# A macaron block of float32 attentions: the order of the steps is written anew, and the exponentials' scales come from registers

## The reference

```python
x = x + 0.5 * ffn_int(norm(x))       # rows quantised to int8, times a 128x128 int8 weight, plus bias
x = x + attn0(norm(x))               # 16 heads of 8, rotary, causal, one W_O of 128x128
x = x + 0.5 * ffn_int(norm(x))
x = x + 0.5 * ffn_gated(norm(x))     # silu(x Wg) * (x Wu), hidden size 384, then Wd
x = x + attn1(norm(x))               # 16 heads of 64, causal, w_o of 1024x128
x = x + 0.5 * ffn_gated(norm(x))
```

## Time and profile before

| | us |
|---|---|
| median of 3 timed runs | 776.01 |
| the three | 773.67, 776.34, 776.01 |
| span of the profiled execution | 771.9 |
| TensorE busy (PE) | 708.9 (92%) |
| VectorE busy (DVE) | 533.9 (69%) |
| ScalarE busy (ACT) | 460.9 (60%) |
| GpSimd busy (POOL) | 488.1 (63%) |

### The profile page before, as it was taken

The page is one execution under the profiler, slowest core; times in us unless marked ns, Lnnn a source line. Parts: engine busy times, 40 slices in busy tenths (PEclk is TensorE's granted clock), DMA queues, the critical chain, the costliest instruction groups (busy, mean ns, idle before and its releaser), DMA issues.

```text
span 771.9 us, 21579 instructions
## 1 busy us (share of the span) xinstructions
PE 708.9 (92%) x9387; PEld 421.0 (55%) x9387; DVE 533.9 (69%) x730; ACT 460.9 (60%) x544; POOL 488.1 (63%) x387
## 2 busy tenths in 40 slices
PE   2768988988888899999999999999999999999997
PEld 1533535445444464666555565655785655666764
DVE  7599889888988786777957556774446465653137
ACT  2424877987787879555565654745525656764502
POOL 6824546206853400689898889969649778889640
PEclk9855999999999999999999999999999999999999
DMA  8000000000000000001011001110101100111000
GB/s 280 2 1 2 4 1 3 3 2 3 3 2 3 1 3 2 2 3 31 3 29 29 30 3 30 31 30 3 29 3 29 31 4 28 29 31 43 27 18 28
DMA packets 13225, 16.20 MB, mean 21 GB/s; under 512 B 3052, under 2 KB 10572, under 8 KB 13132
## 3 DMA queue, kind: packets, MB, share of 16 engines
q1 hardware_dynamic: 12556, 14.50, 6.5%
q10 hardware_dynamic: 576, 0.33, 0.1%
HBM read 13.26 MB, written 1.17 MB: 19 GB/s over the span
## 4 chain that ended last, share of the span: by engine, by line
PE 73%; DVE 11%; ACT 8%; issue 3%; POOL 3%; DMA 1%; SPq 0%; ACTq 0%; DVEq 0%; POOLq 0%
PE ps L1284 21%; PE ps L1233 17%; DVE big L1097 7%; ACT Pr L714 6%; PE ps L1204 6%; PE ps L1263 6%; PE ps L1450 6%; PE ps L1489 3%; PE ps L1457 3%; PE ps L1294 2%; PE ps L1399 2%; PE ps L1274 1%; PE ps L1244 1%; PE ps L1407 1%; PE ps L1254 1%
## 5 line engine op out<-in xcount | busy, mean ns | idle before, releaser
L714 ACT ACTIVATE Pr<-ps,exp_scale 128x1024 f32<-128x1024 f32 (+1 forms) x284 | 277.0, 1032 | 111.2 <-PE ps L1284 54.8
L696 POOL TENSOR_TENSOR V0s<-V0s,Pr 128x1024 f32<-128x1024 f32 x77 | 181.4, 2356 | 94.4 <-PE ps L1233 58.7
L1128 DVE TENSOR_REDUCE mxb<-ps 128x8 f32<-128x1024 f32 (+1 forms) x152 | 173.6, 1163 | 95.3 <-PE ps L1284 75.1
L1097 DVE TENSOR_REDUCE big<-ps 128x8 f32<-128x1024 f32 (+1 forms) x159 | 170.6, 1117 | 18.4 <-PE ps L1263 15.7
L1284 PE MATMUL ps<-big 64*128 64x128 f16 (+2 forms) x2560 | 169.2, 260 | 0.7 <-ACT Pr L714 0.4
L1263 PE MATMUL ps<-big 32*128 32x128 f16 (+2 forms) x1280 | 104.7, 275 | 33.9 <-DVE big L1097 16.5
L1284 PEld LDWEIGHTS ps<-big 64*128 64x128 f16 x2560 | 93.3, 94 | 73.7 <-issue 23.6
L1233 PE MATMUL ps<-Pr,V1s 128*64 128x128 f32 (+2 forms) x960 | 110.5, 371 | 0.0
L1263 PEld LDWEIGHTS ps<-big 32*128 32x128 f16 x1280 | 42.9, 94 | 107.8 <-ACT Pr L714 43.9
L696 POOL TENSOR_TENSOR acts<-acts,Pr 128x1024 f32<-128x1024 f32 x35 | 83.2, 2378 | 18.7 <-PE ps L1233 8.4
L1204 PE MATMUL ps<-Pr,V0s 128*18 128x128 f32 (+2 forms) x1280 | 77.8, 368 | 0.2 <-ACT Pr L721 0.2
(11 more groups left out here) (246 smaller groups left out, 911.7 us busy)
## 6 DMA issues: line engine op xcount, KB each, us to landing
rec_b<-scratch_dram SPq DMA_DIRECT2D x30, 256.0 KB, 3.9
X<-in_x_dram SPq DMA_DIRECT2D x2, 256.0 KB, 3.5
big<-in_pick_rows_dram SPq DMA_DIRECT2D x2, 256.0 KB, 3.0
X<-in_x_dram SPq DMA_DIRECT2D x1, 512.0 KB, 5.3
rec_b<-in_w_q_dram SPq DMA_DIRECT2D x1, 512.0 KB, 5.8
XT<-in_w_k_dram SPq DMA_DIRECT2D x1, 512.0 KB, 6.6
XT<-in_w_v_dram SPq DMA_DIRECT2D x1, 512.0 KB, 7.4
wo_s<-in_w_o_dram SPq DMA_DIRECT2D x1, 512.0 KB, 8.0
```

What stands on the lines that cost most here:

```text
L696: g.tensor_tensor(dst, dst, src, ALU.add).then_inc(summed, 1)
L714: ins = a.activation(dst[:, part], src, func, scale=scale)
L1097: ins = v.tensor_reduce(maxima_of(mall[:, r, 2 * u:2 * u + 2][:, part], i), block_view(src, i), AX.X, ALU.max, negate=True)
L1128: ins = v.tensor_reduce(maxima_of(mxb[:, r][:, part], arg), block_view(src, arg), AX.X, ALU.max, negate=True)
```

## The change

Three edits.

The string `ORDER` is another one. It has the same letters in the same numbers; each stream's own order is what it was. In the string, uninterrupted runs of `W` are 57 instead of 84, the longest has 7 instead of 6.

Three numbers are loaded from SBUF into registers of ScalarE: the scale of the first attention's exponentials when the first `a` is done, that of the second's and the values' factor at the first weight split. The exponentials and the values' copies take their scale from these registers instead of from the 128 partitions.

Before the first weighing of each pair TensorE also waits for ScalarE's copy of that pair's values; in the new order this copy may stand behind the pair's first exponential.

```diff
 ORDER = (
-    "ammmmmmmmammmmmmmmmmamtmmmeeehemmhhememmmwmhewemewemewemhwmemwememehemwthweahemeweehmwegemwemehmwmem"
-    "emwemwemhmewmmhmemmewhmeeemhmwmmhmmtmhhhmememwmeehmegewemmwhmhehwmemheweamewemmtewemewmemwemeemwmeme"
...
-    "TKWWWMEhEEMWWMMQhVWEMMhWWMEEEEEMWWSMEEWWTVKVhWhMWMEMhWMEEMWWMEEEESEMWWWMEMWWWThWEEEEWWWOOSEEEEEOOWWW"
+    "ammmmmmmmammmmmmmmmmmtammheeemehwmemwhememmehewemewmemwmmwehmememehmemwtheahwmeehwemewemegemewmemwe"
+    "memwmehhmewmmhmememmehwememwmhmthmwmhmhhmememwmehewemgeemhmwhemhwmeehwmeamewememtemwemememwmemwemwem"
...
+    "EEEWMMWWMEEEEEMWWWWWWEMhMWWMMKhQVVSTMEEEEEEEEMWWWWMMMWWWEMMWWMEEMhSTEEEEEEWWWWWWWEEEEEESEEWWOOOOWWWW"
     "WWW"
 )
...
+            exp_by = [a.alloc_register(f"exp_by_{k}") for k in range(2)]
+            v_by = a.alloc_register("v_by")
             copy_heads(0)
...
                 if kind == "wsplit":
                     act.wait_ge(scale_ready, 2)
+                    if key == 0:
+                        a.load(exp_by[1], exp_scale[1][0:1, 0:1].bitcast(I32))
+                        a.load(v_by, v_back[0:1, 0:1].bitcast(I32))
...
                     if key == 0:
                         copy_heads(1)
+                        a.load(exp_by[0], exp_scale[0][0:1, 0:1].bitcast(I32))
...
-                    copy_whole(n, group_buf[e_no % GROUP_BUFS], ACT.Exp, exp_scale[0][:, 0:1])
+                    copy_whole(n, group_buf[e_no % GROUP_BUFS], ACT.Exp, exp_by[0])
...
-                    copy_whole(n, in_banks(V1s[:, key % SETS]), ACT.Copy, v_back[:, 0:1])
+                    copy_whole(n, in_banks(V1s[:, key % SETS]), ACT.Copy, v_by)
...
-                    copy_whole(n, dst, ACT.Exp, exp_scale[1][:, 0:1])
+                    copy_whole(n, dst, ACT.Exp, exp_by[1])
...
                 pe.wait_ge(slot_act, read("A", "exp", p, c))
                 if c == 0:
+                    pe.wait_ge(slot_act, read("A", "pv", p, None))
                     pe.wait_ge(acc1_saved if p else acc0_saved, p or G)
```

More of the change, by code:

```diff
@@ L189 @@
 ORDER = (
-    "ammmmmmmmammmmmmmmmmamtmmmeeehemmhhememmmwmhewemewemewemhwmemwememehemwthweahemeweehmwegemwemehmwmem"
-    "emwemwemhmewmmhmemmewhmeeemhmwmmhmmtmhhhmememwmeehmegewemmwhmhehwmemheweamewemmtewemewmemwemeemwmeme"
[L192 to L198, removed]
-    "TKWWWMEhEEMWWMMQhVWEMMhWWMEEEEEMWWSMEEWWTVKVhWhMWMEMhWMEEMWWMEEEESEMWWWMEMWWWThWEEEEWWWOOSEEEEEOOWWW"
+    "ammmmmmmmmammmmmmmmmmmtammheeemehwmemwhememmehewemewmemwmmwehmememehmemwtheahwmeehwemewemegemewmemwe"
+    "memwmehhmewmmhmememmehwememwmhmthmwmhmhhmememwmehewemgeemhmwhemhwmeehwmeamewememtemwemememwmemwemwem"
+    "amewemewemewememewemewemmeewhmmwtmemwhmegememwemegmahhmmwmheheweehmwmemwemhmheewemewemetmehmemwmemwm"
+    "emhahwememhehewemewemewmememwemwemhemheetwemhhhhhwhhhwhhwhemhemgmehemwemheewhemwememememwemwemwemewm"
+    "mhemwmKQQtVVMegeeMweMeweMeweMeweMeweMeweMeweeMgeewTKKQwwMMgEEEMWMMWWMMVhMEEMEEEEMMWWMMKQhTWWWWhMEhSM"
+    "EhEhMWWMhEEMEEMEMWTEMMWWWWMMEWWhMEVhKQWWMEEMhEEMMWWWWTSMhEEEEhMWMMKVQWWMEEEEMWMMMWWWMESTMEMWMEEEMKhQ"
+    "WWMhhhWWEMEEEMTShhhWWWMhEEEEEVhhhWWWMMMhWhWWMEEEMWWMEEMhQKVSTMhhEEEMWWWWWWMEMWMEMWMEEEhWWMMQKWSTEMEE"
+    "EEMWMMQKVWMMMWWWMEEMEEMMWWMMSTWMEEEEEQVKMMWWWWWWMEEMEEMTSMEEMWWMMMWWWWWMEEEMWWMEEEEEEESTVKOOQOOMMMWW"
+    "WWhWWMEEMQKVVMMWWhWMEEMEEEEMSTMEMWWMMMWWWWMEEKhQWWWMEEMEEMhhhhWWWMEETSMEMWhMMMWWWMEEMVhhQVKhhhWWSTME"
+    "EEEWMMWWMEEEEEMWWWWWWEMhMWWMMKhQVVSTMEEEEEEEEMWWWWMMMWWWEMMWWMEEMhSTEEEEEEWWWWWWWEEEEEESEEWWOOOOWWWW"
     "WWW"
```

## The result

The changed kernel takes 770.39 us in the median of eight runs, beside 776.02 for eight runs of the kernel before. One of the eight, of 828.18 us at a mean granted clock of 0.83 instead of 0.96, is left out of the ratio; the other seven lie between 764.92 and 772.6, with a median of 768.7. The ratio is 0.9911, with a 95% interval of [0.9889, 0.9933]: 6.9 us less, where 8.5 were forecast (767.5). The profiled execution has a span of 765.6 us, 6.3 less than before.

What follows compares the result with a forecast made beforehand. TensorE was taken to bound the pair attention, with no engine full in the group attention; -4.7 - 3.2 - 0.3 - 1.0 + 0.2 + 0.5 = -8.5 us from 776.0 gave 767.5 us, range 761.5 to 774.

Steps and rivals of the forecast that it cites:

- Shape changes, pair stage: Pair attention: 49 fewer changes of tile shape on TensorE at 0.096 us each, 4.7 us saved, wholly on the path.
- No new waits: Pair attention: the new order's longer runs of E and M open no waits on TensorE; 0, bound 2 us.
- rival (b): Pair attention: GpSimd's adds become the bound, ScalarE waits at six places, 15 us, giving 782.5 us; chance 0.05.
- Registers: ScalarE's scale from a register saves 94 ns per exponential: 3.2 us in the group attention, hidden in the pair stage.
- The offset of 4.1 us: The profiled span, 771.9 us, lies 4.1 below the timed median of 776.0, which includes what lies around the span.
- Group order: Group attention: 0.3 us from 8 fewer shape changes, 1.0 from fewer bank waits (bounds -3 and +4).
- Tail: Last pair: GpSimd's seven adds, 17.6 us against TensorE's 17.3, end late, so the last sum waits: +0.5 us.
- Loads: Three loads into ScalarE's registers, one early and two at the group attention's first weight split: +0.2 us, from 0 to 3.4.
- (a): Rival: ScalarE's saving buys nothing, by the register form's cost or VectorE's maxima ending last; 771.5 us, chance 0.22.
- (d): Rival: the register form costs 94 ns more per exponential instead of less; 778 us, no change, chance 0.08.
- (e): Rival: the order buys nothing on TensorE, the shape-change surcharge being a wait that only moves; 772.2 us, chance 0.04.
- (c): Rival: the group stage gains 6 us beyond the sum from faster exponentials and the order together; 761.5 us, chance 0.11.

Runs made afterwards that it cites:

- registers only: The kernel before with its old order, plus the three loads and scales from registers; 769.94 us, ratio 0.9924.
- Before, again: The kernel before, unchanged, run once more for a second trace; 775.53 us (one run).
- the swaps: Registers and old order, with W and the M behind it exchanged at 20 pair-stage points, 39 more shape changes; 776.73 us, ratio 1.0003.
- tail mended: Registers, old group order, new pair order, with the last pair's first two weighings moved ahead of its last two score products; 768.18 us, ratio 0.9899.
- three places mended: That mended-tail kernel, plus the ninth pair's sum three steps later and a projection behind two weighings; 769.30 us, ratio 0.9911.
- the order alone: The new order with scales still read from the partitions, against the kernel before; 779.04 us, ratio 1.0037.

## Why the prediction came out right, point by point

The total was forecast well (8.5, measured 6.9), partly because errors of its terms cancelled. Beside the forecast of registers -3.0 and order -5.5 stand, from kernels of one group, registers -6.1 and order -1.0.

- **Shape changes, pair stage: right mechanism, sized too low.** Forecast 49 x 0.096 = 4.7 us; measured 0.12 to 0.14 each, 6.1 to 6.6. The surcharge I read was that between the last matmul of one shape and the first of the next. The weighing behind a change is itself slower: counted over the trace of the pair stage, in weighings of four matmuls of 512 columns, the median from the first to the last is 0.487 us, and 0.436 behind another weighing. The new order has 26 fewer weighings behind a change: 26 x 0.051 = 1.3 us on top of the 4.7. Starts at one boundary don't show that; whole steps do. My check by the sum of the steps' own times had the excess already inside those times.
- **No new waits: wrong, the step that failed.** I took 0 with a bound of 2; beside registers only it is 3.4 us (2.9 between the rows), and 0.68 at the tail. The spot of rival (b) is real, in small: the exponential at 403 us waits for an add. I had called the closest add ready 0.4 us in time; this one was 1.1 late. The rest is smaller waits of one reader each. In sum, the order gave 6.1 to 6.6 and took 3.6 to 4.1.
- **Registers: the duration right, what it is worth too low.** -90 ns for -94 forecast; the earlier trace rows carried it. Group stage -2.8, with 2 us more at low clock, for -3.2. Missed: 1.4 us in the pair stage, where TensorE had small waits, and some 2 us that before's own profile hid. It was the fastest of that kernel's runs (773.67). "Before, again", near the median, has 6 us more at low clock and starts the pairs 2.0 us later; registers only takes 4.7 + 1.3 = 6.0 us off that one, and 6.1 is the difference of the medians.
- **The offset of 4.1 us** that I put around the span: the profiled executions' times are 1.8 above their spans. The other 2.3 was this execution's luck.
- **Group order: wrong in sign or nothing** (forecast -1.3, bounds +4; measured +1.1, not separable from 0). The clock, below, is what I had not priced.
- **Tail: right.** +0.5 forecast (17.6 less 17.3, the two figures that it is made of, are 0.3), 0.68 in the rows. **Added wait: right**, it ended last nowhere. **Loads:** no gap at their places; their price isn't told apart.
- **Rivals.** (a) falls with registers only: ScalarE's saving was the larger part. VectorE did take over the chain (22.1%), but didn't cancel it. (d) falls with 1027 ns, (e) with the swaps. (c) didn't come. Of (b)'s 15 us some 1.3 came, at one place, and with that wait mended VectorE made TensorE wait 1.1 there. Not among them was that the two parts need each other: without the faster exponentials the pair stage gains nothing by the order, and the kernel loses 3.0 us, with its clock lower.

The signs I named came out: 1023 ns (1027), the pair stage 459 to 461 (460.8), the first projections 3 to 5 us earlier (2.3, short of it). TensorE stayed over 98% busy in the pair stage (212.36 of 215 us at the lowest), but the wait for GpSimd that I named as a sign of failure is there at one place.

## What to carry to other kernels

Where a stage is full, price a reordering by whole steps beside and away from a change of tile shape, not by the gap at the boundary, and then run the new order against the readers' times: what the engine saves appears as waits where cover was thin. An order is tuned to the durations of its instructions; a shorter instruction and a new order should be tried apart and together. And before the terms are summed, ask for the median execution, not the one that was profiled: here 2.3 us lay between them.

## What the runs showed of the hardware

**A scale from a register costs what an immediate does.** 1027 and 600 ns against 1023 and 598 for copies without any; one on the partitions makes it 1117, a second operand of that kind 1209. The Trainium skill, page "ScalarE: Activation LUTs", section on what a table load costs, has about 93 ns for each such operand, a bias included; the trace agrees (90 and 92). No run here shows more of it than these two.

**A change of shape goes by the tile that a product is placed in.** The turn of a pair's maxima is one matmul that uses 16 columns, but is placed in the whole array. In the traces before and after, a product of the whole array (128 columns) starts 109 to 114 ns after it (once 153), one in tiles of 32 or 64 columns or of 64 rows 202 to 210 ns. So the turn costs nothing beside a projection and a full change beside the rest, though in both cases the columns in use change. By the columns in use there are 59 fewer changes of shape in the pair stage; ten of them are a turn beside the whole array, and the other 49 are those of the prediction.

**TensorE's clock falls in the stage with waits, at other times in each execution.** In the group stage the granted clock drops to 0.5 for 3.4 or 6.8 us, once 10.2. Between the first pair's start and the last sum, where TensorE is busy 98% and more, it falls in none of the fourteen executions. Two kernels with the same order up to 390 us differ in it there; first the one with the tail mended, then the one with three places mended, 200 to 207 and 80 to 270 us:

```profile
200.00:207.00 7.00, 7.00 (x90) 3.27 (x86) 4.21 (x6) 3.02 (x4) 6.42 (x9) 0.51 0.01 2
...
80.00:270.00 190.00, 166.12 (x2670) 88.79 (x2668) 166.65 (x231) 144.36 (x183) 92.25 (x97) 0.98 0.01 3
```

```profile
200.00:207.00 7.00, 6.44 (x119) 3.05 (x117) 6.61 (x10) 4.58 (x6) 6.51 (x8) 1.00 0.01 2
...
80.00:270.00 190.00, 165.65 (x2720) 89.79 (x2722) 169.40 (x233) 144.96 (x184) 91.82 (x96) 1.00 0.01 3
```

The pairs start at 274.65 and 272.06: 2.6 us apart, of which 0.4 are there at the first exponential already (65.27 and 64.88). So 6.8 us at half clock cost 2.2 to 2.6. With the new group order it falls more often, here the changed kernel, and again:

```profile
80.00:270.00 190.00, 168.70 (x2692) 89.05 (x2684) 170.54 (x244) 144.43 (x177) 93.06 (x98) 0.97 0.01 3
```

```profile
80.00:270.00 190.00, 169.87 (x2682) 90.08 (x2684) 169.63 (x242) 144.54 (x177) 93.67 (x98) 0.96 0.01 3
```

Over whole spans, thirteen runs of the changed kernel average a clock of 0.961, eighteen of the three kernels with the old group order and the new pairs 0.967; a line through either set gives about 4.5 us for 0.01. At one clock the new order would be 1.7 us ahead; at its own it is level within 1 us (medians 768.8 and 768.5). That the waits of the new order are what makes the clock fall is my reading of it; no run here changed the one without the other. In most kernels the slower runs are those with the lower clock, over a spread of up to 9 us (the order alone); medians of six such runs don't tell 1 us.
